# Key stacks written as whole rows, zeros included, from a padded scratch copy

## The chip, the cores and the metric

The kernel runs on one core of one Trainium2 chip. The metric is the device time of one execution in microseconds, the median of several runs. Times inside the kernel come from one profiled execution.

## The reference

One transformer layer over 128 sequences of 64 tokens with 128 channels: a cross-attention with 16 heads of 8 channels each, and then a gated feed-forward part. Cut to what matters here:

```python
q = (Q @ Wq.T + bq).reshape(B, S, H, D_H).transpose(0, 2, 1, 3)     # Q: layernorm(x)
k = (K @ Wk.T + bk).reshape(B, S, H, D_H).transpose(0, 2, 1, 3)     # K: the context
scores = jnp.einsum('bhqd,bhkd->bhqk', q, k) * inv_sqrt_dh
attn = jax.nn.softmax(scores, axis=-1)
ctx = jnp.einsum('bhqk,bhkd->bhqd', attn, v)
...
x = x + ctx @ Wo.T + bo
x = x + ffn(layernorm(x))       # two gates over 128 channels, top 32 of each, two products with one weight
```

## The kernel before

The 128 sequences are worked on in 16 groups of eight (four pairs, 512 tokens). The kernel has two phases. The attention phase takes the first 300 us or so; the gates, with their search for the 32 largest, take the rest. The change is in the attention phase alone.

To get float32 scores out of bf16 matmuls, queries and keys are each cut into three bf16 parts (`q_parts`, `k_parts`), and the parts are stacked along the partition axis, so that one matmul over 96 rows (`MROWS`) sums six products of parts. The stacks are `qst` (128 partitions x 16 heads x 256 tokens, 8 KB of bf16 in a partition) and `kst` (128 partitions x 16 heads x 4 pairs x 2 sequences x 64 tokens, 16 KB in a partition). In `kst` the rows of the first sequence of a pair hold zeros in the place of the second, and the other way round: this keeps the two sequences of a pair apart in one matmul. Four more rows (`MROWS` to `KROWS`) take the row maxima into the matmul; the keys have -1 there (`minus_rows`). There are three stacks of each kind (`STACKS`), used in turn.

The way of the keys of a group: TensorE projects them, ScalarE writes `k32`, GpSimd cuts them into `k_parts` in four operations (`split_keys`), SyncE's queue writes the parts to a scratch in HBM (`write_parts`), and when these writes have landed it reads them back into the stack in another order (`stack`): for each of the two sequences `a` of a pair three DMAs, of 24, 16 and 8 rows (`RUNS`), six for the keys of a group and six for its queries. The queries go the same way with `q_parts`. In the key stack a row is written in 64 pieces of 64 tokens, 128 bytes each, since between two pieces lie the zeros of the other sequence. These zeros are laid once, ahead of the loop: VectorE clears `kst[0]` and `kst[2]`, GpSimd clears `kst[1]`.

All engines run a loop over `t`, a group per step, in an order written out by hand; each waits on semaphores. SyncE's queue has in step `t`: the loads of context (`load_ctx`) and of x (`load_x`) for later groups, the stacks of group `t + 1`, then the scratch writes of group `t + 2`:

```python
                if there(t + 1):

                    wait(sp, act_mT, 2 * t)
                    wait(sp, pe_col, 8 * (t - 1))
                    stack(t + 1, k_scratch, k_out, k_moved, True)
                    stack(t + 1, q_scratch, q_out, q_moved, False)
                if there(t + 2):
                    write_parts(t + 2, k_parts, k_scratch, k_out, k_moved)
                    write_parts(t + 2, q_parts, q_scratch, q_out, q_moved)
```

TensorE has in step `t`, interleaved, the scores of group `t` for the row maxima (`query_side`, line 389), the scores of group `t - 1` for the exponentials (`key_side`, line 345), the product with the values (`values`, line 360), the projections of later groups (`keys` 409, `queries` 415, `values_in` 421) and transposes. `query_side(t, 0)` waits for both stacks of group `t` (`q_moved`, `k_moved`). The row maxima reach `qst` through a small DMA that ScalarE issues (`max_out`, line 692), for which `key_side` waits.

Of the kernel before, what the change touches and what calls it, by code (L numbers as in the profile page):

```python
# [7 lines left out]
F32 = mybir.dt.float32  # L8
BF16 = mybir.dt.bfloat16
ALU = mybir.AluOpType  # L10
# [45 lines left out]
def build(nc, x, ctxT, wq, wk, wv, wo, bqk, bv, bo, bf, ffn_w, conv, gate_cols, lin_w, ident, minus_rows, ones_row, marks, steps, out):  # L56
    with ExitStack() as ctx:
# [24 lines left out]
        k_parts = sb("k_parts", [128, PARTS, GTOK], BF16)  # L82
# [58 lines left out]
        k_scratch = [nc.dram_tensor(f"k_scratch{s}", (2, PARTS, 128, HALF), BF16).ap() for s in range(2)]  # L141
# [55 lines left out]
        gp_zero = sem("gp_zero")  # L197
# [44 lines left out]
        def _(sp):  # L242
# [20 lines left out]
            sp.dma_start(gates[2 * GATES:2 * GATES + 1, :], ones_row).then_inc(rest_in, 16)  # L263
            for s in range(STACKS):

                if s == 1:
                    sp.wait_ge(gp_zero, 1)
                else:
                    sp.wait_ge(dve_zero, s // 2 + 1)
                if s == 2:  # L270
                    load_x(2)
                sp.dma_start(kst[s][MROWS:KROWS, :, :, :, :].rearrange("r h p a m -> r (h p a m)"), minus_rows).then_inc(rows_in, 16)

            def write_parts(g, parts, scratch, done, moved):
                s = g % 2
                if parts is k_parts:
                    wait(sp, gp_split, 4 * g + 4)
                else:
                    wait(sp, dve_split, 4 * min(g + 1, 2))
                    wait(sp, gp_qsplit, 4 * (g - 1))  # L280
                if g >= 2:

                    wait(sp, moved[slot(g - 2)], STACK * uses(g - 2))
                for a in range(2):
                    sp.dma_start(scratch[s][a].rearrange("n c t -> c n t"),  # L285
                                 parts[:, :, a * HALF:(a + 1) * HALF]).then_inc(done[s], 16)

            def stack(g, scratch, done, moved, to_keys):
                s, d = g % 2, slot(g)
                wait(sp, done[s], WRITES * (g // 2 + 1))  # L290
                for a in range(2):
                    for n in RUNS:
                        first = PARTS - n if to_keys else 0
                        src = scratch[s][a, first:first + n].rearrange("n (i h) t -> (n i) (h t)", h=HEADS)
                        rows = spread(a, n)
                        dst = (kst[d][rows, :, :, a, :].rearrange("r h p m -> r (h p) m") if to_keys
                               else qst[d][rows, :, :].rearrange("r h t -> r (h t)"))
                        if to_keys:
                            src = src.rearrange("r (x m) -> r x m", m=SEQ)
                        sp.dma_start(dst, src).then_inc(moved[d], 16)  # L300

            for t in range(FIRST, LAST + 1):
# [4 lines left out]
                if there(t + 1):  # L307
# [3 lines left out]
                    stack(t + 1, k_scratch, k_out, k_moved, True)  # L311
                    stack(t + 1, q_scratch, q_out, q_moved, False)
                if there(t + 2):
                    write_parts(t + 2, k_parts, k_scratch, k_out, k_moved)
                    write_parts(t + 2, q_parts, q_scratch, q_out, q_moved)
# [563 lines left out]
        def _(dve):  # L879
# [71 lines left out]
            dve.memset(kst[0][:, :, :, :, :].bitcast(F32).rearrange("r h p a m -> r (h p a m)"), 0.0).then_inc(dve_zero, 1)  # L951
            for t in range(FIRST - 1, LAST + 2):
# [44 lines left out]
                if t == FIRST:  # L997
                    dve.memset(kst[2][:, :, :, :, :].bitcast(F32).rearrange("r h p a m -> r (h p a m)"), 0.0).then_inc(dve_zero, 1)
# [91 lines left out]
        def _(pool):  # L1090
# [33 lines left out]
            def split_keys(g):  # L1124
                wait(pool, act_k, g + 1)
                if g >= 1:
                    wait(pool, k_out[(g - 1) % 2], WRITES * ((g - 1) // 2 + 1))
# [198 lines left out]
```

## Time and profile before

| | us |
|---|---|
| median of 3 runs | 551.03 (544.9 to 552.81) |
| the profiled execution, its own time | 555.29 |
| its span, first to last instruction | 553.5 |
| outside the span | 1.8 |
| busy PE / DVE / ACT / POOL | 412.1 / 418.0 / 379.4 / 404.9 |
| DMA, whole span | 53.03 MB in 138971 packets, mean 96 GB/s |

A busy time is a share of the whole span, over two phases with different limits. In the attention phase, slices 1 to about 22 of the profile's 40, the DMA engines are in use nearly all the time; in the second phase hardly. A matmul's end is modelled, so a busy PE is not one at its peak.

### The profile page before, as it was taken

To read this page: it belongs to the slowest core of one execution; us is meant where nothing else is said; L and a number is where in the kernel's file an instruction comes from. 1 tells how busy PE (TensorE), PEld (TensorE's weight loads), DVE (VectorE), ACT (ScalarE), POOL (GpSimd) and SP (SyncE) were. 2 spreads that over 40 slices of the span, in tenths; PEclk is the share of its full clock that TensorE was granted. 3 is DMA by queue.
4 is the path that set the end of the run, shared out by engine and by line. 5 is a ranking of instruction groups with operands and counts; after the bars stand their busy time and mean duration, and the time that the engine had idled before them with its cause. 6 is when DMAs were issued, how large, how long until landed. Compare 5 with 4: busy or idle time off the path is not lost.

```text
span 553.5 us, 16382 instructions
## 1 busy us (share of the span) xinstructions
PE 412.1 (74%) x5501; PEld 324.2 (59%) x5516; DVE 418.0 (76%) x1941; ACT 379.4 (69%) x1054; POOL 404.9 (73%) x544
## 2 busy tenths in 40 slices
PE   3458889989999999999989353567666666666663
PEld 1125777767867777779877042555545445555553
DVE  7554677777757777665743479999999999999963
ACT  3424678777877888764653368677877777777774
POOL 7356588767767778761144542899999999999995
PEclk9999999999989999995975555777888887777775
DMA  5788787788878787887000000000000000000002
GB/s 149 160 204 207 173 191 181 180 201 191 205 193 195 175 203 158 181 183 167 5 5 1 1 0 1 2 1 21 20 20 21 21 20 21 20 21 20 21 19 76
DMA packets 138971, 53.03 MB, mean 96 GB/s; under 512 B 105146, under 2 KB 131195, under 8 KB 137339
## 3 DMA queue, kind: packets, MB, share of 16 engines
q1 hardware_dynamic: 136712, 51.47, 38.5%
q8 instruction: 44, 0.72, 0.6%
q10 hardware_dynamic: 2176, 0.52, 0.4%
q14 instruction: 39, 0.32, 0.2%
HBM read 34.67 MB, written 16.78 MB: 93 GB/s over the span
## 4 chain that ended last, share of the span: by engine, by line
SPq 33%; POOL 21%; DVE 17%; PE 12%; issue 9%; DMA 6%; ACT 1%; POOLq 0%; DVEq 0%; ACTq 0%
SPq L300 27%; DVE kst L1056 6%; DVE tops L1046 6%; POOL pT L1215 5%; DMA k_scratch<-k_parts 5%; PE ps_pv L360 4%; SPq L285 4%; POOL x2n L1187 3%; POOL kst L1244 3%; POOL kst L1217 2%; POOL kst L1224 2%; POOL kst L1238 2%; PE ps_col L345 2%; SPq L247 1%; SPq L251 1%
## 5 line engine op out<-in xcount | busy, mean ns | idle before, releaser
L896 DVE TENSOR_REDUCE m<-ps_row 128x8 f32<-128x512 f32 x128 | 82.4, 686 | 59.0 <-PE ps_row L389 59.0
L651 ACT ACTIVATE pT<-ps_col 128x512 f32<-128x512 f32 x128 | 68.6, 587 | 32.8 <-PE ps_col L345 32.8
L1046 DVE MAX8 tops<-kst 128x8 f32<-128x128 f32 x384 | 78.1, 282 | 0.0
L360 PE MATMUL ps_pv<-vx,pT 128*64 128x18 f32 x2048 | 77.9, 219 | 0.0
L360 PEld LDWEIGHTS ps_pv<-vx,pT 128*64 128x64 f32 x2048 | 71.4, 148 | 7.6 <-issue 4.5
L1056 DVE MATCH_REPLACE8 kst<-tops,kst 128x128 f32<-128x128 f32 x264 | 69.5, 282 | 0.0
L563 PE MATMUL ps_pv<-idb,kst 128*128 128x128 bf16 x120 | 14.8, 300 | 72.6 <-ACT kst L791 72.6
L563 PEld LDWEIGHTS ps_pv<-idb,kst 128*128 128x128 bf16 x120 | 11.0, 135 | 76.3 <-ACT kst L791 76.3
L389 PE MATMUL ps_row<-kst,qst 96*64 96x128 bf16 x1024 | 43.4, 230 | 9.8 <-DMA qst<-q_scratch 9.7
L345 PEld LDWEIGHTS ps_col<-qst,kst 100*128 100x128 bf16 x1024 | 36.0, 101 | 23.7 <-issue 12.7
L1215 POOL TENSOR_SCALAR pT<-pT 128x512 bf16<-128x512 bf16 x30 | 44.8, 1493 | 5.0 <-ACT pT L809 5.0
L345 PE MATMUL ps_col<-qst,kst 100*128 100x64 bf16 x1024 | 43.9, 199 | 6.0 <-DMA qst<-mT 5.9
L389 PEld LDWEIGHTS ps_row<-kst,qst 96*64 96x64 bf16 x1024 | 34.0, 117 | 14.1 <-DMA qst<-q_scratch 12.2
L1100 POOL TENSOR_SCALAR ve<-ag 128x4 f32<-128x4 f32 x31 | 7.2, 233 | 47.0 <-DVE ag L888 44.8
L1217 POOL TENSOR_TENSOR kst<-kst,pT 128x512 f32<-128x512 f32 x30 | 34.6, 1155 | 2.5
L1103 POOL TENSOR_TENSOR rs<-ve,half_neg 128x4 f32<-128x4 f32 x31 | 32.1, 1037 | 4.5
L656 ACT ACTIVATE x2n<-xr,nm,rs 128x128 f32<-128x128 f32 x64 | 26.4, 484 | 9.8 <-POOL nm L1107 7.6
L553 PE MATMUL ps_proj<-wf_sb,x2T 128*128 128x128 f32 x128 | 31.4, 424 | 1.3 <-ACT x2T L814 1.3
L883 DVE BATCH_NORM_STATS2 st<-xr 128x6 f32<-128x128 f32 x128 | 27.7, 279 | 4.0 <-DMA xr<-in_x_dram 3.4
L553 PEld LDWEIGHTS ps_proj<-wf_sb,x2T 128*128 128x128 f32 x128 | 28.3, 324 | 1.6 <-ACT x2T L814 1.6
L1129 POOL CAST k_parts<-k 128x512 bf16<-128x512 f32 x16 | 9.8, 610 | 25.6 <-issue 19.8
L656 ACT ACTIVATE xn<-xr,nm,rs 128x128 f32<-128x128 f32 x64 | 26.3, 490 | 3.0 <-POOL nm L1107 3.0
(156 smaller groups left out, 1248.1 us busy)
## 6 DMA issues: line engine op xcount, KB each, us to landing
k_scratch<-k_parts SPq DMA_DIRECT2D x32, 192.0 KB, 2.9
q_scratch<-q_parts SPq DMA_DIRECT2D x32, 192.0 KB, 3.2
kst<-k_scratch SPq DMA_DIRECT2D x32, 192.0 KB
qst<-q_scratch SPq DMA_DIRECT2D x32, 192.0 KB
xr<-in_x_dram SPq DMA_DIRECT2D x16, 256.0 KB, 3.8
cT<-in_ctxT_dram SPq DMA_DIRECT2D x16, 256.0 KB, 3.7
kst<-k_scratch SPq DMA_DIRECT2D x32, 128.0 KB
qst<-q_scratch SPq DMA_DIRECT2D x32, 128.0 KB
```

Of the source, the lines that this page charges most:

```text
L300: sp.dma_start(dst, src).then_inc(moved[d], 16)
L345: mm = pe.matmul(ps_col[pp][:, hh, :], k_cols(s, KROWS, h, p), qst[s][0:KROWS, h, p * SEQ:(p + 1) * SEQ], start=True, stop=True)
L360: mm = pe.matmul(pv_flat[pp * SEQ:(pp + 1) * SEQ, h * 2 * VW:(h + 1) * 2 * VW], pT[:, 2 * j + pp, hh, :], vx[s][:, 2 * hp + pp, h, :], sta ...
L389: mm = pe.matmul(ps_row[b % 2][pp * SEQ:(pp + 1) * SEQ, hh, :, :], qst[s][0:MROWS, h, p * SEQ:(p + 1) * SEQ], k_cols(s, MROWS, h, p), star ...
L553: mm = pe.matmul(ps_proj[:, p * DIM:(p + 1) * DIM], x2T[:, p * 128:(p + 1) * 128], wf_sb[:, :], start=True, stop=True)
L651: act.activation(pT[:, b % PT_RING, :, :], ps_col[b % 2][:, :, :], ACT.Exp, scale=SCALE).then_inc(act_exp, 1)
L656: ins = act.activation(dst[:, p, :], xr[:, PAIRS * g + p, :], ACT.Identity, bias=nm[:, n:n + 1], scale=rs[:, n:n + 1])
L896: dve.tensor_reduce(m32[:, b // 4, :, 4 * j:4 * j + 4].rearrange("q a h -> q h a"), ps_row[b % 2][:, :, :, :], AX.X, ALU.max).then_inc(dve ...
L1046: ins = dve.max(top[:, n, :], src)
L1056: ins = dve.match_replace(picked[s][:, p, cols], top[:, n, :], src, PICKED)
L1215: pool.tensor_scalar(ones_there[:, pairs, :], chosen[g % 2][:, pairs, :], 0.0, None, ALU.is_gt).then_inc(g2_ones, 1)
L1217: pool.tensor_tensor(expd[g % 3][:, pairs, :], expd[g % 3][:, pairs, :], ones_there[:, pairs, :], ALU.mult).then_inc(g2_gate, 1)
```

## The change

The zeros now travel with the keys. GpSimd writes the three parts of the keys into `k_frames`, a buffer in SBUF in which 64 tokens of keys and 64 tokens of zeros take turns; VectorE clears it once. For the second sequence of a pair the same buffer is read from an offset of 64 tokens. The scratch in HBM doubles in length per row (`GTOK` for `HALF`), and each row of the stack is read back in one piece of 16 KB. The clearing of the three `kst` buffers goes away, and with it `gp_zero` and the waits for it. The stack's function is now one for keys and queries. The three `minus_rows` copies follow each other without a wait, and `load_x(2)` follows them.

```diff
@@ -79,7 +79,9 @@
         q_rest = sb("q_rest", [128, GTOK])
         k_rest = sb("k_rest", [128, GTOK])
         q_parts = sb("q_parts", [128, PARTS, GTOK], BF16)
-        k_parts = sb("k_parts", [128, PARTS, GTOK], BF16)
+        k_frames = sb("k_frames", [128, 2 * (PARTS * GTOK + SEQ)], BF16)
         vx = [sb(f"vx{s}", [128, PAIRS, HEADS, 2 * VW]) for s in range(2)]
         pT = sb("pT", [128, PT_RING, HEADS // 2, SEQ])
         attn = sb("attn", [128, 2, 2, DIM])
@@ -138,7 +140,9 @@
                      for g in range(GROUPS)]
         q_scratch = [nc.dram_tensor(f"q_scratch{s}", (2, PARTS, 128, HALF), BF16).ap() for s in range(2)]
-        k_scratch = [nc.dram_tensor(f"k_scratch{s}", (2, PARTS, 128, HALF), BF16).ap() for s in range(2)]
+        k_scratch = [nc.dram_tensor(f"k_scratch{s}", (2, PARTS, 128, GTOK), BF16).ap() for s in range(2)]
+        k_parts = [k_frames[:, :].rearrange("c (a x) -> c a x", a=2)[:, :, n * GTOK:(n + 1) * GTOK]
+                   .rearrange("c a (p m) -> c a p m", p=PAIRS)[:, :, :, 0:SEQ] for n in range(PARTS)]
         xsT = q32
         yin = k32[:, :].rearrange("q (p c) -> q p c", p=PAIRS)
         tops = [sb(f"tops{s}", [128, 2 * PAIRS, TOPK]) for s in range(2)]
@@ -194,7 +198,6 @@
         dve_ab, dve_ve2, dve_nm2 = sem("dve_ab"), sem("dve_ve2"), sem("dve_nm2")
         gp_rs1, gp_rs2, gp_split, gp_xb, gp_bn = (sem(f"gp_{n}") for n in ("rs1", "rs2", "split", "xb", "bn"))
-        gp_zero = sem("gp_zero")
         p2_x2T, p2_lin, p2_full, p2_xsT, p2_yin = (sem(f"p2_{n}") for n in ("x2T", "lin", "full", "xsT", "yin"))
         p2_sidesT, p2_order, p2_aheadT = sem("p2_sidesT"), sem("p2_order"), sem("p2_aheadT")
@@ -261,43 +264,43 @@
                              (wf_sb, ffn_w), (lin_sb, lin_w), (bf_row, bf), (marks_sb, marks), (steps_sb, steps)):
                 sp.dma_start(dst[:, :], src).then_inc(rest_in, 16)
             sp.dma_start(gates[2 * GATES:2 * GATES + 1, :], ones_row).then_inc(rest_in, 16)
             for s in range(STACKS):
-                if s == 1:
-                    sp.wait_ge(gp_zero, 1)
-                else:
-                    sp.wait_ge(dve_zero, s // 2 + 1)
-                if s == 2:
-                    load_x(2)
                 sp.dma_start(kst[s][MROWS:KROWS, :, :, :, :].rearrange("r h p a m -> r (h p a m)"), minus_rows).then_inc(rows_in, 16)
-            def write_parts(g, parts, scratch, done, moved):
+            load_x(2)
+            def write_keys(g):
                 s = g % 2
-                if parts is k_parts:
-                    wait(sp, gp_split, 4 * g + 4)
-                else:
-                    wait(sp, dve_split, 4 * min(g + 1, 2))
-                    wait(sp, gp_qsplit, 4 * (g - 1))
+                wait(sp, gp_split, 4 * g + 4)
                 if g >= 2:
-                    wait(sp, moved[slot(g - 2)], STACK * uses(g - 2))
+                    wait(sp, k_moved[slot(g - 2)], STACK * uses(g - 2))
                 for a in range(2):
-                    sp.dma_start(scratch[s][a].rearrange("n c t -> c n t"),
-                                 parts[:, :, a * HALF:(a + 1) * HALF]).then_inc(done[s], 16)
-            def stack(g, scratch, done, moved, to_keys):
+                    sp.dma_start(k_scratch[s][a].rearrange("n c t -> c n t"),
+                                 k_frames[:, a * PARTS * GTOK:(a + 1) * PARTS * GTOK].rearrange("c (n t) -> c n t", n=PARTS)
+                                 ).then_inc(k_out[s], 16)
+            def write_queries(g):
+                s = g % 2
+                wait(sp, dve_split, 4 * min(g + 1, 2))
+                wait(sp, gp_qsplit, 4 * (g - 1))
+                if g >= 2:
+                    wait(sp, q_moved[slot(g - 2)], STACK * uses(g - 2))
+                for a in range(2):
+                    sp.dma_start(q_scratch[s][a].rearrange("n c t -> c n t"),
+                                 q_parts[:, :, a * HALF:(a + 1) * HALF]).then_inc(q_out[s], 16)
+            def stack(g, scratch, out, moved, stacks, first_part):
                 s, d = g % 2, slot(g)
-                wait(sp, done[s], WRITES * (g // 2 + 1))
+                wait(sp, out[s], WRITES * (g // 2 + 1))
                 for a in range(2):
                     for n in RUNS:
-                        first = PARTS - n if to_keys else 0
-                        src = scratch[s][a, first:first + n].rearrange("n (i h) t -> (n i) (h t)", h=HEADS)
-                        rows = spread(a, n)
-                        dst = (kst[d][rows, :, :, a, :].rearrange("r h p m -> r (h p) m") if to_keys
-                               else qst[d][rows, :, :].rearrange("r h t -> r (h t)"))
-                        if to_keys:
-                            src = src.rearrange("r (x m) -> r x m", m=SEQ)
-                        sp.dma_start(dst, src).then_inc(moved[d], 16)
+                        first = first_part(n)
+                        sp.dma_start(stacks[d][spread(a, n)],
+                                     scratch[s][a, first:first + n].rearrange("n (i h) t -> (n i) (h t)", h=HEADS)).then_inc(moved[d], 16)
+            kst_rows = [kst[s][:, :, :, :, :].rearrange("r h p a m -> r (h p a m)") for s in range(STACKS)]
+            qst_rows = [qst[s][:, :, :].rearrange("r h t -> r (h t)") for s in range(STACKS)]
             for t in range(FIRST, LAST + 1):
                 if 2 <= t + 3 < GROUPS:
@@ -308,11 +311,11 @@
                     wait(sp, act_mT, 2 * t)
                     wait(sp, pe_col, 8 * (t - 1))
-                    stack(t + 1, k_scratch, k_out, k_moved, True)
-                    stack(t + 1, q_scratch, q_out, q_moved, False)
+                    stack(t + 1, k_scratch, k_out, k_moved, kst_rows, lambda n: PARTS - n)
+                    stack(t + 1, q_scratch, q_out, q_moved, qst_rows, lambda n: 0)
                 if there(t + 2):
-                    write_parts(t + 2, k_parts, k_scratch, k_out, k_moved)
-                    write_parts(t + 2, q_parts, q_scratch, q_out, q_moved)
+                    write_keys(t + 2)
+                    write_queries(t + 2)
             for g in range(GROUPS):
                 if g < GROUPS - 1:
@@ -948,7 +951,7 @@
             dve.memset(half_neg[:, :], -0.5).then_inc(dve_half, 1)
             dve.memset(nothing[:, :], 0.0).then_inc(dve_half, 1)
-            dve.memset(kst[0][:, :, :, :, :].bitcast(F32).rearrange("r h p a m -> r (h p a m)"), 0.0).then_inc(dve_zero, 1)
+            dve.memset(k_frames[:, :].bitcast(F32), 0.0).then_inc(dve_zero, 1)
             for t in range(FIRST - 1, LAST + 2):
                 if there(t - 1):
                     row_max(t - 1, 6)
@@ -995,7 +998,6 @@
                 if t < 0:
                     first_stats(t + 4)
                 if t == FIRST:
-                    dve.memset(kst[2][:, :, :, :, :].bitcast(F32).rearrange("r h p a m -> r (h p a m)"), 0.0).then_inc(dve_zero, 1)
                     for s in range(2):
                         dve.memset(vx[s][:, :, :, :].rearrange("k p h v -> k (p h v)"), 0.0).then_inc(dve_frame, 1)
                     dve.wait_ge(dve_frame, 2)
@@ -1125,14 +1127,17 @@
                 wait(pool, act_k, g + 1)
                 if g >= 1:
                     wait(pool, k_out[(g - 1) % 2], WRITES * ((g - 1) // 2 + 1))
+                else:
+                    pool.wait_ge(dve_zero, 1)
+                keys, rest = [b[:, :].rearrange("c (a p m) -> c a p m", a=2, p=PAIRS) for b in (k32, k_rest)]
                 wait(pool, gp_split, 4 * g)
-                pool.tensor_copy(k_parts[:, 2, :], k32[:, :]).then_inc(gp_split, 1)
+                pool.tensor_copy(k_parts[2], keys).then_inc(gp_split, 1)
                 wait(pool, gp_split, 4 * g + 1)
-                pool.tensor_tensor(k_rest[:, :], k32[:, :], k_parts[:, 2, :], ALU.subtract).then_inc(gp_split, 1)
+                pool.tensor_tensor(rest, keys, k_parts[2], ALU.subtract).then_inc(gp_split, 1)
                 wait(pool, gp_split, 4 * g + 2)
-                pool.tensor_copy(k_parts[:, 1, :], k_rest[:, :]).then_inc(gp_split, 1)
+                pool.tensor_copy(k_parts[1], rest).then_inc(gp_split, 1)
                 wait(pool, gp_split, 4 * g + 3)
-                pool.tensor_tensor(k_parts[:, 0, :], k_rest[:, :], k_parts[:, 1, :], ALU.subtract).then_inc(gp_split, 1)
+                pool.tensor_tensor(k_parts[0], rest, k_parts[1], ALU.subtract).then_inc(gp_split, 1)
             def split_queries(g):
                 wait(pool, act_q, g + 1)
@@ -1146,7 +1151,6 @@
                 wait(pool, gp_qsplit, 4 * (g - 2) + 3)
                 pool.tensor_tensor(q_parts[:, 2, :], q_rest[:, :], q_parts[:, 1, :], ALU.subtract).then_inc(gp_qsplit, 1)
-            pool.memset(kst[1][:, :, :, :, :].bitcast(F32).rearrange("r h p a m -> r (h p a m)"), 0.0).then_inc(gp_zero, 1)
             pool.wait_ge(dve_half, 1)
             for t in range(FIRST, LAST + 1):
                 if there(t + 3):
```

SyncE's queue, from the end of the constants' loads to the first group's stacks, kernel before (`4x8192` are the rows of -1; `x2` means two in a row):

```order
L272 DMA kst<-in_minus_rows_dram 4x8192 x2
L247 DMA xr<-in_x_dram 128x512
L272 DMA kst<-in_minus_rows_dram 4x8192
L247 DMA xr<-in_x_dram 128x512
L285 DMA k_scratch<-k_parts 128x3x256 x2
L285 DMA q_scratch<-q_parts 128x3x256 x2
L251 DMA cT<-in_ctxT_dram 128x512
L247 DMA xr<-in_x_dram 128x512
L300 DMA kst<-k_scratch 24x64x64
L300 DMA kst<-k_scratch 16x64x64
L300 DMA kst<-k_scratch 8x64x64
```

The same place in the changed kernel:

```order
L269 DMA kst<-in_minus_rows_dram 4x8192 x3
L250 DMA xr<-in_x_dram 128x512 x2
L279 DMA k_scratch<-k_frames 128x3x512 x2
L290 DMA q_scratch<-q_parts 128x3x256 x2
L254 DMA cT<-in_ctxT_dram 128x512
L250 DMA xr<-in_x_dram 128x512
L299 DMA kst<-k_scratch 24x8192
L299 DMA kst<-k_scratch 16x8192
L299 DMA kst<-k_scratch 8x8192
```

The third copy of -1 rows moves ahead of the load of x. The key writes take 512 tokens per part in place of 256. The key stack's copies have two dimensions in place of three. The order within a step of the loop stays.

VectorE from its start to the first queries' split, kernel before:

```order
L951 MEMSET kst 128x4096
L883 BN_STATS st<-xr 128x6 x4
L888 BN_AGGR ag<-st 128x2 x4
L883 BN_STATS st<-xr 128x6 x4
L888 BN_AGGR ag<-st 128x2 x4
L998 MEMSET kst 128x4096
L1000 MEMSET vx 128x1152 x2
```

The same place in the changed kernel:

```order
L954 MEMSET k_frames 128x1600
L886 BN_STATS st<-xr 128x6 x4
L891 BN_AGGR ag<-st 128x2 x4
L886 BN_STATS st<-xr 128x6 x4
L891 BN_AGGR ag<-st 128x2 x4
L1002 MEMSET vx 128x1152 x2
```

Of two clearings of 4096 words one of 1600 is left. GpSimd's own clearing of `kst` is gone too.

## Rows read from the trace of the kernel before

**Rows 1.** The page, part 4: chain that ended last, by engine and line.
```profile
SPq 33%; POOL 21%; DVE 17%; PE 12%; issue 9%; DMA 6%; ACT 1%; POOLq 0%; DVEq 0%; ACTq 0%
...
SPq L300 27%; DVE kst L1056 6%; DVE tops L1046 6%; POOL pT L1215 5%; DMA k_scratch<-k_parts 5%; PE ps_pv L360 4%; SPq L285 4%; POOL x2n L1187 3%; POOL kst L1244 3%; POOL kst L1217 2%; POOL kst L1224 2%; POOL kst L1238 2%; PE ps_col L345 2%; SPq L247 1%; SPq L251 1%
```

**Rows 2.** Timeline of SyncE's queue, step t = 5: start us, us, what, count.
```profile
115.60 6.15 SPq L300 DMA_DIRECT2D kst<-k_scratch  x6
121.80 3.98 SPq L300 DMA_DIRECT2D qst<-q_scratch  x6
125.88 1.05 SPq L285 DMA_DIRECT2D k_scratch<-k_parts  x2
127.05 1.41 SPq L285 DMA_DIRECT2D q_scratch<-q_parts  x2
128.50 0.57 SPq L251 DMA_DIRECT2D cT<-in_ctxT_dram  x1
129.11 0.50 SPq L247 DMA_DIRECT2D xr<-in_x_dram  x1
129.78 7.37 SPq L300 DMA_DIRECT2D kst<-k_scratch  x6
```

**Rows 3.** Timeline of PE at four places: start us, us, what [idle before <-releaser].
```profile
36.55 1.06 PE L389 MATMUL ps_row<-kst,qst 96*64 96x128 bf16 x16 [2.92 <-DMA qst<-q_scratch]
...
114.05 0.64 PE L389 MATMUL ps_row<-kst,qst 96*64 96x128 bf16 x16 [1.70 <-DMA qst<-q_scratch]
...
115.09 1.10 PE L415 MATMUL ps_proj<-xnT,wq_sb 128*128 128x512 f32 x2
...
125.87 0.64 PE L345 MATMUL ps_col<-qst,kst 100*128 100x64 bf16 x16 [0.30 <-DMA qst<-mT]
...
129.84 1.10 PE L415 MATMUL ps_proj<-xnT,wq_sb 128*128 128x512 f32 x2
...
237.42 1.10 PE L415 MATMUL ps_proj<-xnT,wq_sb 128*128 128x512 f32 x2
```

**Rows 4.** DMA packets of 117.9:123.3, the key stack.
```profile
DMA packets 5931, 0.77 MB, mean 142 GB/s; under 512 B 5930, under 2 KB 5930, under 8 KB 5930
```

**Rows 5.** DMA packets of 124.9:126.9, the query stack.
```profile
DMA packets 79, 0.38 MB, mean 189 GB/s; under 512 B 33, under 2 KB 33, under 8 KB 33
```

**Rows 6.** DMA packets of 113:115.5, the scratch writes.
```profile
DMA packets 1472, 0.72 MB, mean 287 GB/s; under 512 B 114, under 2 KB 1471, under 8 KB 1471
```

**Rows 7.** DMA packets of 116.2:117.6, loads of context and x.
```profile
DMA packets 278, 0.42 MB, mean 303 GB/s; under 512 B 73, under 2 KB 74, under 8 KB 278
```

**Rows 8.** Windows, query stack, writes, loads: the last columns are PEclk, DMA share, GB/s.
```profile
core 0: us, PE busy (x) PEld busy (x) DVE busy (x) ACT busy (x) POOL busy (x), PEclk, DMA share, GB/s
124.20:127.20 3.00, 2.70 (x69) 2.42 (x66) 1.74 (x4) 2.38 (x7) 2.75 (x5) 1.00 0.71 210
128.40:130.40 2.00, 2.00 (x54) 1.67 (x52) 1.26 (x4) 1.26 (x4) 1.21 (x4) 1.00 0.94 261
130.80:132.00 1.20, 1.20 (x23) 1.03 (x23) 1.20 (x5) 1.20 (x3) 1.14 (x2) 1.00 0.84 281
```

**Rows 9.** The page, part 3: DMA queues.
```profile
q1 hardware_dynamic: 136712, 51.47, 38.5%
q8 instruction: 44, 0.72, 0.6%
```

**Rows 10.** Line 300, the stacks' issues: duration ns min/median/max.
```profile
L300 SPq DMA_DIRECT2D kst<-k_scratch x96: 657/782/3047, 24.0 to 256.3; - x96
L300 SPq DMA_DIRECT2D qst<-q_scratch x96: 518/618/1888, 29.9 to 260.3; - x96
```

**Rows 11.** The chain in order of time, start: start us, us, what.
```profile
1.70 3.47 DVE kst L951
5.18 0.74 DVE st L883 x4
...
9.68 3.48 DVE kst L998
...
14.81 9.16 DMA k_scratch<-k_parts
```

**Rows 12.** Waits: PE for the small copies; GpSimd ahead of the keys' split.
```profile
POOL k_parts L1129 <- issue: 19.8, 12, 3.7
...
PE ps_col L345 <- DMA qst<-mT: 5.9, 10, 1.8
```

**Rows 13.** Windows, columns as in rows 8: the first with a slower TensorE clock behind step 13.
```profile
237.00:262.00 25.00, 24.01 (x400) 20.83 (x399) 15.26 (x45) 13.43 (x28) 10.23 (x14) 0.74 0.78 169
```

## The prediction

> **What bounds the kernel now.** I read the chain of waits first. Issues of line 300, the stacks' copies, are 27% of the span on it, by far its largest line, and nearly all of the attention phase [rows 1]. The timeline of SyncE's queue says why: in one step it spends 6.15 us on six key copies, 3.98 us on six query copies, 1.05 and 1.41 us on the scratch writes, 0.57 and 0.50 us on two loads, and after 14.2 us, at 129.78, the next step's key copies follow without a pause [rows 2]. Then TensorE. Its step, from line 415 to line 415, was 14.75 us here (115.09 to 129.84), with 0.30 us of waiting in it, so its own work is about 14.45 us. The step before had a wait of 1.70 us for the stacks ahead of line 389 [rows 3]. From 37.54 (first row of line 415 right behind the one at 36.55) to 237.42 line 415 runs for 14 groups, so 13 steps in 199.9 us, 15.4 us each. So two queues lie within a microsecond of each other: TensorE could do a step in 14.45 us, and the way of the stacks takes 15.4.
>
> The third is the one that the chain doesn't name: the DMA engines. I cut a step into stretches by what they carry. Key stack: 142 GB/s, nearly all packets of 128 bytes [rows 4]; its 768 KB (0.786 MB) take 5.5 us. Query stack: 189 to 210 GB/s for as many bytes in 8 KB pieces, 3.7 to 4.2 us [rows 5, 8]. Scratch writes of keys and queries, together 0.786 MB in pieces of 512 bytes, at 287 GB/s: 2.7 us [rows 6]. Two loads, 0.52 MB, at 303 GB/s: 1.7 us [rows 7]. Sum 13.6 to 14.1 us of the 15.4, one stretch after the other. The DMA engines are thus almost as full as the other two.
>
> **The change part by part.** *SyncE's issues.* Six key copies become of the queries' form. A query copy has a median of 0.618 us and a key copy of 0.782, up to 3.0 [rows 10]; the six cost 3.98 in place of 6.15 us [rows 2]. That is 2.2 us a step off the queue: 14.2 - 2.2 = 12.0 us. SyncE is no longer late, whatever its neighbours do.
>
> *The key stack's transfer.* Packets fall from 6144 to 96 a group, bytes double to 1.57 MB. The fall in packets would be the gain: at 142 GB/s small packets are the slowest traffic in the step. What 1.57 MB costs is the question. Nearest is the query stack, the same rows and the same six copies with rows half as long: 210 GB/s at a share of 0.71 of the sixteen engines [rows 8], which gives 7.5 us; the stretch at 189 GB/s [rows 5] gives 8.3. That the share is 0.71 while the stretch is full of work says that few rows don't fill sixteen engines, and rows of 16 KB are as few. The lower bound is the best rate in a step, the loads' 303 GB/s [rows 7]: 5.2 us. I take 7.5 us, since its row has the same shape: 2.0 us more than now.
>
> *The scratch writes of the keys.* 0.39 MB more, in as many packets of 1 KB. If a packet cost the same, nothing; if a byte does, 0.39 MB at 287 GB/s is 1.4 us. In the stretch of writes one engine carries 261 / (16 x 0.94) = 17.4 GB/s with 512 bytes a piece, in that of loads 281 / (16 x 0.84) = 20.9 with 2 KB [rows 8]. At 19 GB/s an engine, between the two, 0.786 MB take 2.6 us in place of 1.4, at the loads' 20.9 they take 2.35. I take 1.0 more, by the loads' rate, since 1 KB is no longer a small piece.
>
> *The sum of a step on the DMA engines*: 7.5 (keys) + 3.7 (queries, at 210 GB/s) + 2.7 + 1.0 (writes) + 1.7 (loads) = 16.6 us, over TensorE's 14.45 and SyncE's 12.0. Do they run without gaps? The next key stack waits for its scratch write to land, and behind that write the engines still have the query write (1.4 us) and two loads (1.7 us), which cover the way of a new copy; so no gap is added, and I count none. The step goes from 15.4 to 16.6: +1.2 us, over 13 steps +15.6 us. Bounds: 5.2 + 3.7 + 2.7 + 1.7 = 13.3 us, under TensorE's 14.45, which would then be the step; and 8.3 + 4.2 + 4.1 + 1.7 = 18.3 us, +38 us.
>
> *The start.* Three clearings go: 3.47 and 3.48 us on VectorE [rows 11] and GpSimd's. One of 1600 words comes, 3.47 x 1600 / 4096 = 1.4 us. The first sat ahead of the first statistics (5.18), but x comes only about then, so at most 0.2 us is won. The second held back SyncE: the key write of group 0 was issued at about 14.3, and could now go at 12.2, when GpSimd has split the keys. Yet this write landed 9.16 us after its issue [rows 11], with two loads of x and the rows of -1 ahead of it, and these stay ahead. It gains up to 2.1 us and loses 1.4 us for its own doubled bytes; the first stacks then transfer 2.0 us longer, where SyncE's shorter issue gives some back. I count 0, between -2 and +2.
>
> *GpSimd's split.* The four operations now write in pieces of 64 tokens. Should that cost each half as much again, 1.8 us a step, the 19.8 us of idle time in 12 waits ahead of line 1129 [rows 12] cover most of it. *The small copies of the row maxima* share the engines with pieces of 16 KB; TensorE waited 5.9 us for them in ten waits [rows 12]. In the forecast TensorE waits over 2 us a step anyway and they hide; were TensorE the bound, half a microsecond a step could be added. *Behind 237 us* and in the second phase nothing changes.
>
> **The total.** The profiled execution took 555.3 us and would take 571; it is 4.3 us over the median of 551.0, so against the median 551.0 + 15.6 = 566.6, rounded 567 us.
>
> **The rivals.** *1. The large rows run at full rate* and the DMA step falls to 14.45 us or less; TensorE becomes the bound. For it: 128-byte packets are the slowest traffic, and SyncE's queue, now on the chain, loses 2.2 us. Against it: the query stack, with rows of 8 KB, reaches only 210 GB/s. It needs the key stack in 14.45 - 8.1 - 1.0 = 5.3 us, just the lower bound. Time: 0.95 us x 13 = 12 us less, 539 us.
>
> The Trainium skill says what would make this rival true (DMA: Bandwidth & Descriptors, "Specifications"): line rate needs pieces of at least 512 bytes, and an engine moves about 27 GiB/s, by which a 16 KB row takes an estimated 0.57 us. By its section "Why a DMA increments its semaphore by 16 and not by 1" a copy of 24 rows runs on 12 engines, one of 8 rows on 8, so the busiest engines get 8 of a group's 96 rows, an estimated 4.5 us; the step would be TensorE's and the time this rival's 539 us. The rows here show the share of 0.71 that fits such a spread, but 142, 189 and 287 GB/s, not the line rate.
>
> *2. A draw.* The key stack takes 5.7 to 7 us because, with SyncE no longer late, rows of different copies overlap, and the step stays at 14.9 to 16.1. For it: part of the query stretch's 3.98 us is the pace of the issues [rows 2], not of the engines, so 7.5 may be too much. Time 545 to 560, about 552.
>
> *3. Rows of 16 KB are dearer still.* The only pieces of 16 KB in number are the instruction fetches: 44 packets, 0.72 MB, 0.6% of sixteen engines' span [rows 9], 0.006 x 16 x 553.5 / 44 = 1.2 us each. At that price 96 rows at a share of 0.71 take 10.1 us, the step 19.2, +3.8 x 13 = +49: 600 us. Against it: these fetches come singly in the middle of other traffic.
>
> *4. The row isn't moved in one piece* but cut by the hardware: the packets of the first queue would not fall from 136712 [rows 9] by 16 x (6144 - 96) to 39944. Pieces of 2 KB at the loads' 281 GB/s give 5.6 us, so this is a way into rival 2 or 1.
>
> **How the numbers follow.** Forecast, steps of 16.1 to 17.5 us, 560 to 579: 50%. Draw, 545 to 560, with 4 in it: 26%. TensorE as the bound, 536 to 545: 17%. Dearer rows: 7%. The three runs of before lie 1.4% apart, so 2% (540 to 562) is about what can be told from no change. Slower than 562: 0.46 of the forecast and 0.07; faster than 540: 0.13 of the 0.17; within: 0.34. The range takes in the draw and the forecast, part of rival 1 and the dearer half of the bound: 541 to 586.
>
> **What would show it.** Right: line 415 steps of over 16 us with 2 us of waiting for the stacks ahead of line 389; SyncE's queue with pauses ahead of the key stack, where it waits for scratch writes; six key copies issued in about 4 us; the DMA share in the attention phase up and its rate near 240 GB/s in place of 190; a stretch of the key stack of 7 to 8 us. Wrong: steps of 14.5 us with TensorE unbroken (rival 1); a key stretch of 5 to 6 us; or steps above 18. TensorE's clock fell for part of the 25 us behind 237 (mean 0.74 [rows 13]); a fall inside the 13 steps would blur this, and would have to be taken out first.

## The result and the profile after

The changed kernel takes 615.6 us (median of 4 runs, 612.4 to 623.8) where the kernel before takes 550.75 us (544.9 to 552.8) beside it: ratio 1.118, 95% interval 1.106 to 1.129. Slower, as forecast, but by 65 us and not by 16, and far outside the range. The profiled execution took 623.8 us, 68.5 more than the one of before. It is the longest of the four, 8 us over their median, with a mean granted clock of 0.79 over its whole span where the other three had 0.79 to 0.83, so sizes read from it below are those of a long execution.

The windows of the attention phase come first (columns as in rows 8). The changed kernel's 13 steps:

```profile
40.00:300.00 260.00, 210.77 (x3551) 162.25 (x3549) 139.74 (x442) 151.94 (x327) 147.51 (x209) 0.82 0.72 205
```

The same 13 steps of the kernel before:

```profile
37.00:237.00 200.00, 187.23 (x3598) 146.91 (x3595) 139.12 (x445) 150.23 (x328) 147.18 (x209) 0.99 0.81 190
```

The queries' projection (now line 418) runs from 40.54 to 302.12, 20.1 us a step in place of 15.4 [rows 3]: 13 x 4.74 = 61.6 us of the 68.5; it starts 3.0 us later, and some 4 us come behind it. The windows split the 4.7 us a step. TensorE is busy 210.8 / 13 = 16.2 us a step where it was 14.4, for the same matmuls, at a clock of 0.82 in place of 0.99: +1.8. It is idle 49.2 / 13 = 3.8 us where it was 1.0: +2.8. And the DMA share fell, from 0.81 to 0.72. A kernel that is short of DMA engines doesn't use them less.

The page of the changed kernel, parts 3 and 4 (against rows 9 and rows 1):

```profile
q1 hardware_dynamic: 39944, 70.34, 39.8%
...
PE 33%; DMA 19%; DVE 17%; POOL 16%; issue 8%; ACT 3%; SPq 3%; POOLq 0%; DVEq 0%; ACTq 0%
DMA qst<-mT 16%; PE ps_pv L363 8%; DVE kst L1058 7%; DVE tops L1048 7%; PE ps_col L348 6%; POOL pT L1219 4%; PE ps_mix L378 4%; PE ps_proj L412 3%; PE ps_row L392 3%; PE ps_proj L418 3%; POOL x2n L1191 3%; PE ps_proj L424 2%; POOL kst L1248
```

Packets are exactly the 39944 reckoned, so each row travels in one piece. SyncE's queue is gone from the chain (33% to 3%). In its place stands `qst<-mT`, the small DMA of the row maxima, 16 KB. Its waits, between 40 and 330 us (line, what it waited for, us in total, times, longest), beside those of rows 12:

```profile
PE ps_col L348 <- DMA qst<-mT: 47.6, 14, 7.3
```

One such wait, in the chain in order of time (start us, us, what):

```profile
107.57 7.27 DMA qst<-mT
114.84 0.04 issue
114.88 1.04 PE ps_col L348 x16
...
127.62 0.28 ACT mT L691
...
127.94 0.04 issue
127.98 7.48 DMA qst<-mT
135.46 0.05 issue
135.50 1.04 PE ps_col L348 x16
```

From one landing (114.84) to the next issue (127.98) is 13.1 us, TensorE's work nearly all of it; the copy adds 7.5. Together 20.6 us, the step. SyncE's queue there, against rows 2:

```profile
119.55 4.19 SPq L299 DMA_DIRECT2D kst<-k_scratch  x6
123.78 3.89 SPq L299 DMA_DIRECT2D qst<-q_scratch  x6
127.77 0.91 SPq L279 DMA_DIRECT2D k_scratch<-k_frames  x2
129.72 1.77 SPq L290 DMA_DIRECT2D q_scratch<-q_parts  x2
131.54 1.70 SPq L254 DMA_DIRECT2D cT<-in_ctxT_dram  x1
133.28 0.43 SPq L250 DMA_DIRECT2D xr<-in_x_dram  x1
140.17 2.22 SPq L299 DMA_DIRECT2D kst<-k_scratch  x3
```

The copy at 127.98 is issued just behind all twelve stack copies. Then the queue pauses from 133.7 to 140.17. Up to 137.1 the scratch write of the keys hadn't landed yet (such waits: 52.4 us in 14, between 40 and 330 us); what ends the pause is `act_mT` (37.4 us in 14). ScalarE writes that `mT` at 139.88, and its input is TensorE's, which stood behind the small copy. So while TensorE waits no stack is started, and then the stack's data stand ahead of a small copy again.

The DMA queues' packets say more of the 7.48 us (queue, packets, MB, share of 16 engines). q1 carries SyncE's copies, q10 ScalarE's small ones, 68 packets each. From the issue at 127.98 to 132.60, and from there to 135.10:

```profile
q1 hardware_dynamic: 628, 1.22, 90.2%
...
q1 hardware_dynamic: 677, 0.74, 90.2%
q10 hardware_dynamic: 68, 0.02, 3.0%
```

For 4.6 us not one packet of the small copy moves, and then its 68 are spread over 2.4 us among those of q1. The small copy before it, issued at 119.61 when the DMA engines were idle, moved them all between 120.80 and 121.10:

```profile
q10 hardware_dynamic: 68, 0.02, 24.5%
```

Windows of the same step show the price on all sides:

```profile
119.00:121.80 2.80, 2.80 (x63) 2.35 (x62) 1.49 (x5) 1.33 (x4) 2.22 (x3) 0.90 0.32 76
121.80:131.20 9.40, 9.40 (x200) 7.85 (x200) 6.89 (x27) 8.16 (x18) 6.12 (x8) 1.00 0.86 215
131.20:138.00 6.80, 2.80 (x33) 2.33 (x28) 2.27 (x6) 2.73 (x6) 3.41 (x7) 0.65 0.80 265
138.00:142.30 4.30, 4.30 (x69) 2.71 (x68) 2.04 (x7) 1.60 (x4) 2.10 (x3) 0.76 0.19 50
```

The DMA share is 0.19 in the last 4.3 us, before the next stack's data flow. And from 135.5 to 140.5, right behind TensorE's wait, the granted clock was 0.54:

```profile
135.50:140.50 5.00, 5.00 (x55) 3.50 (x55) 1.02 (x2) 1.93 (x4) 0.45 (x1) 0.54 0.36 124
```

That is about the 1.2 GHz level: the keys' projection took 1.92 us there, and the 16 matmuls of line 348 1.04 us in place of 0.64.

### The profile page after: what moved, and what is told of

The parts are those of the page before. It is cut to its first block, busy times and chain, and to the rows that moved or that the text cites. A ratio compares the mean times of both kernels' runs of the same rounds, so it can differ in the third digit from the quotient of the medians.

```text
span 622.0 us, 16381 instructions
## 1 busy us (share of the span) xinstructions
PE 438.1 (70%) x5501; PEld 341.9 (55%) x5516; DVE 413.6 (66%) x1940; ACT 382.1 (61%) x1054; POOL 402.1 (65%) x543
## 3 DMA queue, kind: packets, MB, share of 16 engines
q1 hardware_dynamic: 39944, 70.34, 39.8%
## 4 chain that ended last, share of the span: by engine, by line
PE 33%; DMA 19%; DVE 17%; POOL 16%; issue 8%; ACT 3%; SPq 3%; POOLq 0%; DVEq 0%; ACTq 0%
DMA qst<-mT 16%; PE ps_pv L363 8%; DVE kst L1058 7%; DVE tops L1048 7%; PE ps_col L348 6%; POOL pT L1219 4%; PE ps_mix L378 4%; PE ps_proj L412 3%; PE ps_row L392 3%; PE ps_proj L418 3%; POOL x2n L1191 3%; PE ps_proj L424 2%; POOL kst L1248 2%; POOL kst L1221 2%; DMA k_scratch<-k_frames 2%
## 5 line engine op out<-in xcount | busy, mean ns | idle before, releaser
L363 PE MATMUL ps_pv<-vx,pT 128*64 128x18 f32 x2048 | 84.2, 226 | 2.6 <-issue 1.4
L363 PEld LDWEIGHTS ps_pv<-vx,pT 128*64 128x64 f32 x2048 | 77.6, 158 | 10.1 <-issue 6.4
L348 PE MATMUL ps_col<-qst,kst 100*128 100x64 bf16 x1024 | 49.3, 209 | 47.6 <-DMA qst<-mT 47.6
L348 PEld LDWEIGHTS ps_col<-qst,kst 100*128 100x128 bf16 x1024 | 40.9, 108 | 65.8 <-DMA qst<-mT 49.9
L566 PE MATMUL ps_pv<-idb,kst 128*128 128x128 bf16 x120 | 14.7, 299 | 72.9 <-ACT kst L794 72.9
L1134 POOL CAST k_frames<-k 128x512 bf16<-128x512 f32 x16 | 9.8, 611 | 66.1 <-ACT k L665 59.5
L925 DVE TENSOR_TENSOR xr<-xr,ps_mix 128x256 f32<-128x256 f32 x32 | 13.4, 417 | 56.5 <-PE ps_mix L378 56.5
L392 PE MATMUL ps_row<-kst,qst 96*64 96x128 bf16 x1024 | 44.8, 233 | 7.4 <-DMA qst<-q_scratch 5.8
L412 PE MATMUL ps_proj<-cT,wk_sb 128*128 128x512 f32 x32 | 29.7, 1028 | 8.4 <-DMA wq_sb<-in_wq_dram 5.3
L1146 POOL CAST q_parts<-q 128x512 bf16<-128x512 f32 x14 | 8.6, 611 | 40.7 <-DVE m_parts L907 40.7
L913 DVE RECIPROCAL den<-ps_pv 128x32 f32<-128x32 f32 x32 | 11.0, 345 | 33.1 <-PE ps_pv L363 33.1
```

The lines of the kernel that those rows point to most:

```text
L348: mm = pe.matmul(ps_col[pp][:, hh, :], k_cols(s, KROWS, h, p), qst[s][0:KROWS, h, p * SEQ:(p + 1) * SEQ], start=True, stop=True)
L363: mm = pe.matmul(pv_flat[pp * SEQ:(pp + 1) * SEQ, h * 2 * VW:(h + 1) * 2 * VW], pT[:, 2 * j + pp, hh, :], vx[s][:, 2 * hp + pp, h, :], sta ...
L392: mm = pe.matmul(ps_row[b % 2][pp * SEQ:(pp + 1) * SEQ, hh, :, :], qst[s][0:MROWS, h, p * SEQ:(p + 1) * SEQ], k_cols(s, MROWS, h, p), star ...
L412: pe.matmul(ps_proj[:, :], wk_sb[:, :], cT[g % CTX_RING][:, :, :].rearrange("c p m -> c (p m)"), start=True, stop=True).then_inc(pe_k, 1)
```

## The experiments

Each ratio is to the kernel before, run on the same chip.

**1. Without the small copy.** The row maxima's DMA goes to four spare rows, `key_side` no longer waits for it, and the maxima's rows hold constants (-1 and 0) loaded once. Left out is the subtraction of the maxima.

```diff
-                if j == 0:
-                    wait(pe, m_moved[hp][s], 16 * uses(g))
...
-                act.dma_start(qst[slot(g)][MROWS:KROWS, :, hp * 128:(hp + 1) * 128],
+                act.dma_start(qst[slot(g)][KROWS:KROWS + 4, :, hp * 128:(hp + 1) * 128],
```

> The changed kernel, except that the row maxima's small copy goes to rows of the query stack that no matmul reads, so that nothing waits for it; the four rows of the query stack that held the maxima hold constants from the start, so the maxima are left out of the scores (each softmax is taken without them). Copies, bytes and order of the queues stay. Theory A (the small copy is late behind the 16 KB rows, 7.5 us from issue to landing, and TensorE's wait for it also holds back the next stack): the step falls from 20.4 us to the DMA engines' own 16.6 to 17, about 565 to 575 us. Theory B (the larger bytes alone, the small copy is only the last to be waited for): the wait moves to the stacks and the step stays at 19 to 20 us, over 600.

Measured: 583.1 us, ratio 1.057 (1.042 to 1.071), 17.4 us a step. Half of the loss, 32 us, is gone (35 in the 13 steps; they begin 4.5 us later, behind more copies of constants at the start). The time lies between theory A (565 to 575) and theory B (over 600). What is left stands in this kernel's chain in order of time:

```profile
125.70 9.08 DMA k_scratch<-k_frames
...
144.07 7.51 DMA k_scratch<-k_frames
```

Between these two the chain holds only SyncE's issues: key write, landing, both stacks, next write. So this step is again a loop, of SyncE's 12 issues and of the key write's landing, 7.5 to 9.1 us after its issue, amid the stacks' data. It moves the data at nearly the rate that was forecast. The 13 steps in one window, and TensorE's wait for the stacks:

```profile
45.05:271.39 226.34, 199.73 (x3602) 157.48 (x3601) 141.89 (x447) 151.34 (x329) 147.31 (x209) 0.90 0.83 234
...
PE ps_row L391 <- DMA qst<-q_scratch: 30.1, 13, 5.9
```

234 GB/s (forecast: near 240), 2.3 us of waiting for the stacks in each step (forecast: 2), 17.4 us (forecast: 16.6). In these numbers the kernel that the prediction described is this one, without the small copy.

The same edit in the kernel **before** is its control:

> The kernel before with e1's edit: the small copy of the row maxima goes to rows that no matmul reads, nothing waits for it, and the maxima are left out of the scores. TensorE waited 5.9 us in all for this copy before; so by every theory 544 to 551 us. It shows that the 32 us that e1 gained belong to the small copy's wait in the changed kernel, and not to work that e1 left out.

Measured: 558.9 us (553.5 to 564.4) beside 551.6 (547.8 to 556.8), over the 544 to 551 expected; 15.37 us a step in the profile, as before, but the first of the 13 begins 4.1 us later. The edit gains nothing there, so the 32 us belong to the changed kernel.

**2. Without SyncE's wait for `act_mT`** (the pace), in the changed kernel and in the kernel before.

```diff
-                    wait(sp, act_mT, 2 * t)
```

> The changed kernel without SyncE's wait for act_mT ahead of a stack, so that a key stack is issued as soon as its slot is free and its scratch write has landed. Theory A: the stack starts some 5 us earlier in TensorE's step, its long rows are mostly through when the small copy is issued, and the gap of 3 us without DMA goes; step 16.6 to 18 us, 565 to 590 us. Theory B: the DMA engines work without a gap, 16.6 us a step, about 567. Theory C (the small copy meets a backlog wherever the stack starts): 18 to 20 us a step, 590 to 615.

> The kernel before without SyncE's wait for act_mT ahead of a stack. SyncE's queue was never seen to pause there (14.2 us of issues in steps of 15.4), so every theory expects no change: 545 to 553 us. If it is faster by over 1%, the pace wait cost the kernel before too.

Measured: the changed kernel gets slower, 650.9 us (two executions, 644.6 and 657.2; its own longest without this edit was 623.8), beyond all three theories, and 22.1 us a step in the profile of the longer one; its waits for the small copy rise to 71.3 us in 14. In its chain in order of time:

```profile
125.42 9.22 DMA qst<-mT
...
146.39 9.39 DMA qst<-mT
```

The kernel before doesn't change: 550.3 us, ratio 0.999 (0.995 to 1.003). (Its profile has 15.9 us a step where that of the kernel before has 15.4, with a total 2.1 us shorter: half a microsecond a step is not told from one profile.) That the pause made the step long, my first theory, is refuted: stacks issued earlier put more in front of the small copy (the landings in the chain between 40 and 330 us: 6.0 to 10.7 us, where the changed kernel has 5.8 to 8.5). The pause is a part of the loop, and not its cause.

**3. Pieces of 1 KB**: as many bytes, each row cut into 16 pieces, by a scratch whose rows are padded.

```diff
+                        src = scratch[s][a, first:first + n].rearrange("n (i h) t -> (n i) h t", h=HEADS)
+                        dst = stacks[d][spread(a, n)].rearrange("r (h t) -> r h t", h=HEADS)
```

> The changed kernel with a gap of 128 bytes behind each channel's row in the scratch, so that a row of the key stack arrives in 16 pieces of 1 KB, zeros included; the same bytes in 24576 packets in place of 1536. Theory A: a small copy waits for pieces of 1 KB and not of 16 KB, takes about 3 us as in the kernel before, and TensorE hardly waits for it; step 15.5 to 17 us, 552 to 570. Theory B: bytes unchanged, the small pieces at best as fast: step 20 us or more, 610 or more.

Measured: 633.1 us, ratio 1.147 (1.128 to 1.166), 20.7 us a step, as theory B had it. The small copies in its chain still take 6.1 to 9.5 us (waits 60.2 us in 14). So the size of the pieces is not the reason; what is left is the bulk of the data in front.

**4. The query stack behind the second small copy.** SyncE waits for it between the two stacks, so that it is issued with six copies ahead of it and not twelve.

```diff
                     stack(t + 1, k_scratch, k_out, k_moved, kst_rows, lambda n: PARTS - n)
+                    wait(sp, act_mT, 2 * t + 1)
                     stack(t + 1, q_scratch, q_out, q_moved, qst_rows, lambda n: 0)
```

> The changed kernel, with SyncE waiting for the next maxima (act_mT of 2t + 1) between the key stack and the query stack of a group, so that the small copy is issued when only the key stack is ahead of it and most of that has moved. e2 and e3 have shown that neither an earlier stack nor smaller pieces help the small copy. Theory D (the small copy is served behind everything that was issued before it, whatever its queue): it lands 2 to 4 us after its issue in place of 7.5, TensorE hardly waits for it, and the step is the DMA engines' and the chain's, 17.4 to 18.5 us, 580 to 600 us. Against D: it still takes over 6 us, and the time is 615 or more.

Measured: 590.0 us, ratio 1.073 (1.062 to 1.083), 18.1 us a step. The time is in the range of theory D, but its small copy isn't: it was to land in 2 to 4 us with hardly a wait, and TensorE still waits 29.1 us in 13 for it. Its queue and its chain show both cases in one run. The queue:

```profile
122.15 4.91 SPq L299 DMA_DIRECT2D qst<-q_scratch  x6
...
149.10 4.26 SPq L299 DMA_DIRECT2D kst<-k_scratch  x6
155.03 4.17 SPq L299 DMA_DIRECT2D qst<-q_scratch  x6
```

The chain:

```profile
122.21 4.08 DMA qst<-mT
...
131.72 4.55 DMA qst<-mT
...
140.07 4.05 DMA qst<-mT
...
155.09 9.27 DMA qst<-mT
```

A small copy issued with the query stack, and not behind it, landed after 4.1 us. The one at 155.09, with a key stack and its neighbours issued in the 6 us before it, took 9.3, with the same 16 KB on the same queue of ScalarE. So the stack in front of it is what makes it late.

**5. Only the scratch writes doubled.** Scratch and `k_frames` as changed, the stack read in pieces of 128 bytes without the zeros, the clearings back.

```diff
+                            src = src.rearrange("r (x b m) -> r x b m", b=2, m=SEQ)[:, :, a, :]
+                            dst = kst[d][spread(a, n), :, :, a, :].rearrange("r h p m -> r (h p) m")
```

> The changed kernel's frames, padded scratch and doubled key writes, but the stack reads only the keys, in pieces of 128 bytes as before, and the three stacks are cleared once (all three by VectorE, one after the other, so the start is some us later). It prices the doubled scratch writes alone. By my prediction's term for them, +1.0 us a step if the DMA engines set the step, 564 us and some us for the start; if SyncE's issues set it and the engines have room, no more than the start, 551 to 557.

Measured: 571.4 us, ratio 1.039 (1.030 to 1.049), 16.6 us a step, +1.2. Here VectorE does all three clearings ahead of the loop, and the first of the 13 steps begins 6 us later, 43.69 for 37.54; without that it would be about 565. So the writes cost about 1.2 us a step (forecast: 1.0), and the stack's own doubling the rest, 17.4 - 16.6 = 0.8 us against the slow 128-byte pieces, until the small copy comes into it. Both are differences of single profiles, good to half a microsecond as experiment 2 showed.

**6. Larger pieces without zeros.** In the kernel before, the four pairs' keys become the innermost dimension of `kst`, then two of them. A row's 64 pieces of 128 bytes become 16 of 512, or 32 of 256; TensorE reads its moving operand at a step of 4 elements (8 bytes), or 2.

```diff
-        kst = [sb(f"kst{s}", [128, HEADS, PAIRS, 2, SEQ], BF16) for s in range(STACKS)]
+        kst = [sb(f"kst{s}", [128, HEADS, 2, SEQ, PAIRS], BF16) for s in range(STACKS)]     # 512 bytes
+        kst = [sb(f"kst{s}", [128, HEADS * 2, 2, SEQ, 2], BF16) for s in range(STACKS)]     # 256 bytes
```

> The kernel before with another order inside a key stack's row, head, sequence, token, pair, in place of head, pair, sequence, token: the 256 keys of a head and a sequence lie together, so a row arrives in 16 pieces of 512 bytes, without zeros, in place of 64 of 128; ScalarE writes its keys in this order, and TensorE reads its columns with a step of 4 elements. If pieces of 128 bytes are what makes the stack slow: key stretch of 3.5 to 4 us for 5.5, SyncE's issues 2 us shorter, TensorE the bound at 14.5 to 14.9 us a step, 538 to 545 us. If a step of 4 elements slows TensorE's reads, each matmul of lines 345 and 389 takes longer and the time is over 551.

> The kernel before, with the key stack laid out as [heads*2, 2 (which pair), keys, 2 (k of the pair)]: pieces of 256 bytes, 32 to a row in place of 64 of 128 bytes, no zeros, no rows of 16 KB, the same bytes; TensorE reads the stack at a step of 2 elements (4 bytes) where the layout with 512-byte pieces read it at 4 elements, and ScalarE writes the query's 32 keys in two activations. Theory T (TensorE's read is slowed by the step between elements, and a step of 2 is still free): the score matmuls stay near 220 ns, the wait for the query stack and for the small copy goes, the step falls to 14.5 to 15.0 us, the kernel to 538 to 548 us. Rival U (any step above 1 slows the read): matmuls of 250 to 295 ns, the step 15.3 to 16.5 us, 551 to 562 us. Rival V (halved pieces alone don't shorten the transfer enough): matmuls near 220 ns, a wait of over 0.3 us for the query stack left, 548 to 553 us.

Measured, 512 bytes: 561.1 us, ratio 1.021 (1.014 to 1.028), 16.54 us in each step from the fifth on. There are hardly any waits for stacks left, but the score matmuls got slower (the page, part 5):

```profile
L389 PE MATMUL ps_row<-kst,qst 96*64 96x128 bf16 x1024 | 70.8, 293 | 2.2 <-DMA qst<-q_scratch 2.1
```

Sixteen of them take 1.10 us in place of 0.64 [rows 3], four times a step: 1.8 us. Those of line 345 take 0.72 in place of 0.64, 0.3 us a step. Together that is 16.5 - 14.45. The same row with 256 bytes:

```profile
L389 PE MATMUL ps_row<-kst,qst 96*64 96x128 bf16 x1024 | 43.4, 227 | 2.6 <-DMA qst<-q_scratch 2.6
```

227 ns, 14.7 us a step, and 540.1 us (537.4 to 546.8), ratio 0.983 (0.973 to 0.992). That is 1.7% under the kernel before: packets fall from 136712 to 87560 with the same 51.47 MB, and the step is near TensorE's own 14.45 us. By theory T the wait for the small copy was to go as well; it didn't, it is 10.0 us in 12 in place of 5.9 in ten, and that is most of what is left over 14.45.

## Why the prediction was wrong

**What held.** *SyncE's issues*: six key copies in 4.19 us (forecast 3.98), pauses ahead of the key stack (in part for the scratch write, as forecast, in part for `act_mT`), the queue off the chain. *Packets*: 39944, so rival 4 is out. *Scratch writes*: +1.2 us a step in experiment 5, for +1.0. *The start*: 3.0 us later, just outside -2 to +2. *GpSimd's split*: no wait of TensorE's comes from it. *Rivals 1 and 2* fell. That the time rose, as forecast, is luck by half: the volume of the copies, which the prediction reckoned, is behind 32 of the 65 us, and a wait that it put at nothing behind the other 32. The Trainium skill's rates (DMA: Bandwidth & Descriptors, "Specifications") had spoken for rival 1; the estimate of 0.57 us for a row of 16 KB that they gave is refuted by the measured 1.1 us below.

**The sum of a step was a little low.** With the small copy out, the step is 17.4 us and not 16.6. Of the price of a row the cleanest piece is the first 16 KB pieces of a stack in the changed kernel, 119 to 122 us:

```profile
q1 hardware_dynamic: 12, 0.20, 27.5%
```

0.275 x 16 x 3 us / 12 = 1.1 us a row, near rival 3's price (1.2), not that of the query stack's rate. By the packets of the whole stack its 96 rows took 1.11 us each on average, from 121.3 to 130.6 us, 9.3 us for the 7.5 of the sum. The query stack's rows of 8 KB took 0.43 us each in the kernel before: the prediction carried their rate over to rows of twice the length, which took 2.6 times as long. With 9.3 the sum would be 18.4; the query stack's rows begin at 126.6, ahead of the end of the key stack's, and an overlap of this kind can account for the 1.0 between 18.4 and the measured 17.4. Together the sum was off by 0.8 us a step, 0.8 x 13 = 10 us of the miss. Rival 3's 600 us lies nearest to the measured time, but not by its reason: its step of 19.2 us by volume is not what experiment 1 shows.

**The step that failed** is the sentence on the small copies of the row maxima: "In the forecast TensorE waits over 2 us a step anyway and they hide; were TensorE the bound, half a microsecond a step could be added." Two things in it were wrong. Waiting for stacks and waiting for the small copy don't cover each other: they are at different places of TensorE's order (line 392 and line 348), and the second decides when the next stack may start. And the size: I took "share the engines" to mean a small delay, from 5.9 us in ten waits [rows 12]. With the doubled stack in front the copy lands after 5.8 to 8.5 us in the changed kernel. That gave a loop, 13.1 us of TensorE and 7.5 us of copy, 20.6 us in the step shown (20.1 on average), longer than the sum of any one resource. Experiment 1 takes the copy out: -32 us. Experiment 4 moves half of the queue behind it: -26. These, with the control, show that the wait for the small copy is the cause, and that the stacks in front of it make it long.

**"No gap is added"** failed by the same loop: the DMA engines are nearly idle for some 4 us a step (share 0.19), since the stack's start hangs on TensorE by way of `act_mT`. But experiment 2 shows that to take this gate away alone makes it worse.

**The clock** was named only as a blur. Behind a wait of 4.0 us it was 0.54 for the next 5 us, and the same work took 1.8 us a step more. It goes with the wait: with the small copy out (experiment 1) the clock of the 13 steps was 0.90 in place of 0.82. In this profile, that of a long execution, it is over a third of the loss per step.

**In numbers**, of 4.7 us a step: 2.0 stay with the small copy out, by the larger volume and the loop of the key write (experiment 1: 17.4 - 15.4, of which the writes 1.2), 2.7 are the small copy with the clock behind it.

**What stays open.** Why a copy issued on ScalarE's queue is served behind SyncE's backlog. The Trainium skill (DMA: Bandwidth & Descriptors, "Queues, rings and completion order") says that each DMA engine takes turns between the queues it has work for, a packet at a time, and its packets hold several pieces, typically 9 to 17. By that the copy should wait for a packet or so of the other queue: an estimated 10 us for 9 pieces at the measured 1.1 us, and under 2 us for 17 pieces of 0.1 us. The runs show 4.1 to 5.8 us from its issue to its first piece wherever TensorE waited for it, and with pieces a sixteenth the size 4.1 to 6.4, though these took under 0.1 us each on average. The first fits that rule, the second doesn't. On the other hand the same page ("Issuing engines are not separate DMA queues") says that DMAs of different engines run on the same sixteen and interleave, and that fits the spread of its pieces among those of q1. It isn't one line in the order of issue either: pieces of the query write, issued at 129.72 on SyncE's queue, move from 130.8 on, and the small copy, issued at 127.98, begins at 132.6. The rows of a trace don't name the DMA engine of a piece, so it stays open whether the small copy sits on the engines that have the most rows of the stacks. No run moved it to other partitions or another queue.

## What to carry to other kernels

A sum per resource gives only a lower bound for a step. Follow the shortest DMA that another engine waits for, ask what will be queued ahead of it by the change, and see whether that wait holds back the transfer that causes it: then the latencies add into a loop that no busy share shows, and TensorE's clock falls on top. To make small pieces larger, first look for a layout that joins pieces without more bytes (here two keys side by side, 256 bytes, -1.7%), and check at which step the engine that reads it still keeps its pace.

## What the runs showed of the hardware

- A 16 KB DMA on ScalarE's queue moved its first piece 1.2 us after its issue when the DMA engines were idle. Where the last copy of a stack had been issued 3.6 us or more before (experiment 4) it landed in 4.1 to 4.6 us, and with one or both stacks (1.6 to 2.4 MB) right in front in 5.8 to 10.7 us, whether the pieces there were 16 KB or 1 KB.
- A piece of 16 KB into one partition took 1.1 us, some 15 GB/s, and one of 8 KB 0.43 us, some 19 GB/s; the stretch of the doubled stack (121.8 to 131.2 us) ran at 215 GB/s with a DMA share of 0.86.
- A bf16 moving operand of 128 columns read at a step of 4 elements costs 293 ns a matmul, at a step of 2 elements 227, at a step of 1 230 (the kernel before). The mean of line 345, where the stack is the stationary operand, stayed at about 200 ns in all three, but sixteen of them took 0.72 us at a step of 4 and 0.64 at 1 and 2.
- TensorE's granted clock was 0.54 for the 5 us behind a wait of 4.0 us, and 1.00 in the 9.4 us before it.
